# Attention scores from two-part q and k: two heads stacked in the rows of the array, the diagonal mask on TensorE

## Chip, cores and metric

One core of one Trainium2 chip. The metric is the device time of one launch in microseconds (us), median of the runs shown. Engines are named as in the profile: PE (TensorE matmul), PEld (its weight loads), DVE (VectorE), ACT (ScalarE), POOL (GpSimd), SP (the queue that issues the DMAs).

## What is computed

A macaron block on x of shape 8 x 1024 x 256, all float32:

```python
x = x + 0.5 * ffn(layernorm(x))      # fp4-quantised gate, up and down, hidden 704
x = x + attn(layernorm(x))
x = x + 0.5 * ffn(layernorm(x))

def attn(x):                         # 16 heads of 16 columns
    q, k, v = (heads(x @ W.T) for W in (Wq, Wk, Wv))
    logits = einsum('bhqd,bhkd->bhqk', q, k) * 16 ** -0.5
    logits = where(causal, logits, -max)
    return merge(softmax(logits) @ v) @ Wo.T
```

## The kernel before

Stages in order: weights (split into high and low parts), first feed-forward, the q/k/v projection (`project_qkv`, 16 chunks of 512 rows), attention, then output projection and second feed-forward in one pipeline. The change touches the projection's outputs and attention; the feed-forwards are left alone.

**Operands.** q and k are needed at float32 accuracy. The projection writes each as three bf16 parts (`qkv_parts`: ACT rounds the high part, DVE subtracts into `rest`, ACT rounds the middle part, POOL subtracts the low one) to DRAM. For attention `fill` loads a group of 4 heads of one sequence into a `q_stack` and a `k_stack` with 12 DMAs: 6 pairs of parts x 16 = 96 rows, so that one bf16 matmul with 96 contraction rows gives a head's q.k. Rows 96 and 97 hold minus one in `k_stack` and the row maximum in two bf16 parts in `q_stack`, so the 98-row matmul gives q.k minus the maximum. There is a ring of 4 groups' buffers.

**Order.** 8 sequences x 4 groups = 32 groups, run one after the other by `group(b, g, last)`; sequences 1 to 6 are a hardware loop. Each engine has its own instruction stream and waits on counters (`once`, `wait_ge`); PE executes its stream in order. A group has 12 steps (`STEPS`). Step i takes one 128-row tile of keys against up to 512 queries, in widths 512, 384, 256, 128, then 512, 512, 512, 384, 512, 256, 512, 128 columns. In step i PE does:

- S, the scores of the 4 heads (`score_head`, line 1260): the two heads of pair A into the two banks of `hT_ps`, those of pair B into `av_ps`. Each pair has this one buffer, so the next step's S waits until ACT has taken it;
- V, the values of the step before (`values`, line 1283): 4 heads, float32, `probs` against `v_group`, one head in each 32 columns of the array, into `o_ps` (a bank of `gu_ps`);
- U, units of the row maximum (`max_unit`, line 1243) for the group one or two ahead: q.k again, this time queries on the partitions, into one of three banks (two of `gu_ps`, and `xd_ps`) in strict turn: entry e uses bank e mod 3 and waits (`bank_free`) until entry e - 3 has been consumed. A unit is one matmul of up to 512 columns, or several heads side by side when they are narrow. A group has 39 units; step 0 to 11 carry 5, 3, 2, 1, 4, 5, 4, 3, 5, 2, 4, 1 of them. DVE consumes each unit (`reduce_unit`): a masked maximum (line 1436) for blocks on the diagonal, a plain one (line 1441) elsewhere;
- T, the transposes of finished outputs (`turn_out`, after steps 1 and 5) and one of the maxima (`turn_max`, after V in step 7), which take a bank in the same turn. The outputs are consumed by DVE's `one_over` and `divide` (steps 2 and 6), the maxima by ACT's `m_hi` and DVE's `m_lo` (in step 8, behind the first unit).

ACT makes `probs` from the scores (line 1376, one instruction for both heads of a pair).

**Mask on the diagonal.** In steps 0 to 3 PE adds it: one bf16 matmul of `mask_kq` against an identity for each head (line 1264, 16 in a group). In steps 5, 7, 9 and 11 (`DIAG`) ACT copies the 128-column diagonal block of both heads to `diag_scores` (line 1373), POOL masks it (line 1413), ACT takes the exponential (line 1381), and V waits for that too.

**Before group 0** the maxima of group 0 and part of group 1's are made with nothing else on PE (the loop over `FIRST`).

## Time and profile before

| | us |
|---|---|
| median of 3 runs | 2229.68 (2229.11 to 2231.6) |
| the profiled execution | 2228.96 |
| its span, first to last instruction | 2227.2 |
| first feed-forward and weights | to about 560 |
| q/k/v projection | to about 688 |
| attention | to about 1685 |

Busy shares over the span: PE 94%, DVE 86%, PEld 62%, ACT 59%, POOL 45%. The table of 40 slices shows PE in its top tenths almost throughout, a granted clock of 9 tenths or more save in the first slices and in the one at 668 to 724 us (6 tenths), and POOL near idle in attention.

In the rows, "x4" is a number of instructions merged into one row: start, duration, engine, line, operation, tiles, shapes, count. A float32 matmul has two records. Consecutive matmuls overlap in their durations, so what one costs PE in a stream is the distance of its start to the next start.

### The profile page before, as it was taken

Reading aid. Unit: us, or ns where it says so; the run is one execution under the profiler, and the core shown is the slowest. Engines: PE = TensorE matmul, PEld = TensorE weight load, DVE = VectorE, ACT = ScalarE, POOL = GpSimd, SP = SyncE. Lnnn points to the kernel's source line nnn. Section 1 sums busy time; section 2 is a strip of 40 time slices with the busy share of each in tenths; the row PEclk is TensorE's granted clock in tenths of the full one; section 3 lists DMA queues with packets and bytes.
Section 4 is the critical chain, followed back from the end, with each engine's and each line's share of the span. In section 5 each row is a group of like instructions: output and inputs, shape, how many; then the busy total and the mean of one; then the engine's idle time right before and its main releaser. Section 6 shows DMA issues by size and latency. Waiting matters only on the chain. (4 is left out here: it accounts for less than half of the span.)

```text
span 2227.2 us, 50129 instructions
## 1 busy us (share of the span) xinstructions
PE 2087.8 (94%) x13960; PEld 1374.4 (62%) x13960; DVE 1923.9 (86%) x4807; ACT 1313.3 (59%) x2413; POOL 1005.3 (45%) x1671
## 2 busy tenths in 40 slices
PE   4799999997998999999999999999998799999998
PEld 3688888886883333333333333333336788888887
DVE  6799999996987888888888888988863699999996
ACT  3455555543762777777677777777784344555553
POOL 4788888873654011111011111101110288888884
PEclk7899999998996999999999999999998899999998
DMA  6000000002689665545665546665403100000000
GB/s 210 1 1 0 0 0 0 0 1 71 229 234 181 76 78 72 72 65 70 77 78 66 71 63 77 78 78 67 55 12 122 35 16 19 19 19 19 19 19 25
DMA packets 163272, 133.33 MB, mean 60 GB/s; under 512 B 78432, under 2 KB 138208, under 8 KB 163040
## 3 DMA queue, kind: packets, MB, share of 16 engines
q1 hardware_dynamic: 163104, 131.25, 32.8%
q8 instruction: 86, 1.41, 0.3%
q14 instruction: 82, 0.67, 0.1%
HBM read 79.82 MB, written 51.38 MB: 59 GB/s over the span
## 5 line engine op out<-in xcount | busy, mean ns | idle before, releaser
L1413 POOL TENSOR_SCALAR_AFFINE_SELECT diag_scores<-diag_scores 128x256 f32<-128x256 f32 x256 | 104.1, 406 | 876.9 <-ACT diag_scores L1373 870.9
L1436 DVE CUSTOM_DVE_ANT_0 gu_ps<-gu_ps,mask_qk 128x256 f32<-128x256 f32 (+3 forms) x801 | 372.5, 501 | 33.6 <-PE gu_ps L1243 31.6
L1376 ACT ACTIVATE probs<-hT_ps 128x1024 f32<-128x1024 f32 (+3 forms) x352 | 280.4, 796 | 176.4 <-PE hT_ps L1264 112.8
L1243 PE MATMUL gu_ps<-k_stack,q_stack 96*128 96x512 bf16 (+3 forms) x1121 | 327.1, 331 | 9.9 <-DVE part_max L1436 7.4
L1283 PE MATMUL gu_ps<-probs,v_group 128*17 128x512 f32 (+3 forms) x3072 | 323.1, 493 | 0.7 <-ACT probs L1381 0.6
L713 PE MATMUL gu_ps<-wguT_hi,ffn_xT_hi 128*128 128x512 f32 (+1 forms) x768 | 313.1, 408 | 7.2 <-DVE ffn_xT_lo L589 5.1
L1376 ACT ACTIVATE probs<-av_ps 128x1024 f32<-128x1024 f32 (+3 forms) x352 | 282.1, 801 | 22.3 <-PE av_ps L1260 17.6
L713 PE MATMUL gu_ps<-wguT_hi,ffn_xT_lo 128*128 128x512 f32 (+1 forms) x768 | 290.9, 379 | 0.0
L713 PE MATMUL gu_ps<-wguT_lo,ffn_xT_hi 128*128 128x512 f32 (+1 forms) x768 | 290.7, 379 | 0.0
L691 ACT ACTIVATE ffn_z<-xs,ffn_shift,ffn_rstd 128x256 f32 (+1 forms) x128 | 77.1, 602 | 349.8 <-POOL ffn_shift L642 349.8
L1441 DVE TENSOR_REDUCE part_max<-gu_ps 128x1 f32<-128x512 f32 x320 | 208.3, 683 | 62.9 <-PE gu_ps L1243 62.9
L1260 PE MATMUL hT_ps<-q_stack,k_stack 98*128 98x512 bf16 (+3 forms) x768 | 242.3, 331 | 15.9 <-issue 14.1
L1243 PEld LDWEIGHTS gu_ps<-k_stack,q_stack 96*128 96x128 bf16 x1121 | 96.9, 98 | 220.7 <-DVE part_max L1436 149.1
L1260 PE MATMUL av_ps<-q_stack,k_stack 98*128 98x512 bf16 (+3 forms) x768 | 218.0, 329 | 3.1 <-ACT probs L1376 3.1
L744 PE MATMUL xd_ps<-wdT_hi,ffn_hT_hi 128*128 128x256 f32 x640 | 192.9, 301 | 21.7 <-DVE ffn_hT_lo L528 21.7
L612 POOL TENSOR_TENSOR ffn_hq<-ffn_g_h,ffn_nscale 128x704 f32<-128x704 f32 (+1 forms) x256 | 210.4, 843 | 2.8 <-PE hT_ps L755 2.8
L661 POOL TENSOR_TENSOR ffn_v_h<-ffn_h,ffn_rec 128x704 f32<-128x704 f32 x128 | 178.2, 1393 | 16.3 <-DVE ffn_rec L572 6.7
L744 PE MATMUL xd_ps<-wdT_hi,ffn_hT_lo 128*128 128x256 f32 x640 | 182.7, 285 | 0.0
L744 PE MATMUL xd_ps<-wdT_lo,ffn_hT_hi 128*128 128x256 f32 x640 | 182.7, 285 | 0.0
L713 PEld LDWEIGHTS gu_ps<-wguT_hi,ffn_xT_hi 128*128 128x128 f32 x768 | 146.8, 191 | 26.7 <-DVE ffn_xT_lo L589 7.4
L713 PEld LDWEIGHTS gu_ps<-wguT_hi,ffn_xT_lo 128*128 128x128 f32 x768 | 146.1, 190 | 22.6
L713 PEld LDWEIGHTS gu_ps<-wguT_lo,ffn_xT_hi 128*128 128x128 f32 x768 | 147.3, 192 | 17.3
(215 smaller groups left out, 5084.9 us busy)
## 6 DMA issues: line engine op xcount, KB each, us to landing
q_stack<-q_parts SPq DMA_DIRECT2D x192, 128.0 KB, 6.7
k_stack<-k_parts SPq DMA_DIRECT2D x192, 128.0 KB, 7.5
q_parts<-qkv_parts SPq DMA_DIRECT2D x32, 384.0 KB, 2.7
k_parts<-qkv_parts SPq DMA_DIRECT2D x32, 384.0 KB, 2.8
v_ones<-qkv_vst SPq DMA_DIRECT2D x16, 544.0 KB, 3.8
v_group<-v_ones SPq DMA_DIRECT2D x32, 272.0 KB, 10.6
xs<-in_L_attn_x SPq DMA_DIRECT2D x8, 1024.0 KB, 12.0
attn_rows<-ao SPq DMA_DIRECT2D x64, 128.0 KB, 5.4
```

Of the source, the lines that this page charges most:

```text
L612: last = G.tensor_tensor(blocks(hq[:, to:to + n]), blocks(g_h[:, of:of + n]), spread(nscale[:, par, of // BLK:(of + n) // BLK]), ALU.mult)
L661: G.tensor_tensor(blocks(v_h[:, par, :]), blocks(h[:]), spread(rec[:, OF_H]), ALU.mult).then_inc(s["v_h"], 1)
L691: S.activation(z[:, 1 - par, :], x_tile(i + 5), ACT.Identity, bias=shift[:], scale=rstd[:]).then_inc(s["z"], 1)
L713: last = T.matmul(gu_ps[:, n, 0:cols.stop - cols.start], x[:, buf, k * P:(k + 1) * P], w[:, k, cols], start=k == 0 and m == 0, stop=k == K ...
L744: T.matmul(down_ps, x[:, k * P:(k + 1) * P], w[:, k, :], start=k == 0 and n == 0, stop=False)
L1243: mm = T.matmul(out[:, e, :], qs[0:STACK, h0 + e, t * P:(t + 1) * P], ks[0:STACK, h0 + e, c * CHUNK:c * CHUNK + w], start=True, stop=True)
L1260: mm = T.matmul(scores[pair][:, e, 0:widths[i]], ks[0:STACK_MAX, h, t * P:(t + 1) * P], qs[0:STACK_MAX, h, (j + 1) * CHUNK - widths[i]:(j ...
L1283: mm = T.matmul(o_ps[h * VPAD:h * VPAD + VCOLS, CHUNK - w:CHUNK], vs[:, t, h, :], probs[:, h // 2, i % 2, h % 2, 0:w], start=first, stop=last)
L1376: S.activation(probs[:, pair, i % 2, :, first:w], scores[pair][:, :, first:w], ACT.Exp, scale=DH ** -0.5).then_inc(s[pr], 1)
L1413: G.affine_select(out=block_of, in_=block_of, compare_op=ALU.is_ge, fill=MASKED, base=0, pattern=[[0, 2], [1, P]], channel_multiplier=-1). ...
L1436: last = V.tensor_tensor_reduce(out=ps[:, e * w:(e + 1) * w], in0=ps[:, e * w:(e + 1) * w], in1=mask_qk[:, CHUNK - w:CHUNK], scale=1.0, sc ...
L1441: last = V.tensor_reduce(part_max[:, h0:h0 + per, t, c], ps[:, 0:per * w].rearrange("p (h w) -> p h w", h=per), AX.X, ALU.max)
```

## The change

1. q and k are split into two float32r parts (12 and 12 bits) rather than three bf16 ones. A head's stack is 3 pairs of parts x 16 = 48 rows (+2 for the maximum), float32r. ACT rounds the high part and DVE's subtraction writes the low part; the ACT copies of the middle part and POOL's subtractions are gone.
2. Heads 0, 1 of a group lie at partitions 0 to 63 and heads 2, 3 at 64 to 127 (`HALF`). S of a pair and each unit of the maximum are issued as two matmuls that use the upper and the lower 64 rows of the array and write two different banks. `fill` still issues 12 DMAs of 128 KB and one for v, whose DRAM layout now has one run for each partition. The maximum is stored once and loaded with two DMAs.
3. Units come in twos: both entries' banks must be free before the first of the two matmuls. 40 units; steps 0 to 11 carry 2, 2, 1, 0, 3, 2, 2, 2, 2, 1, 2, 1 twos. Their widths, in order, with the number of heads side by side in each unit: step 0: 2 of 128, 512; step 1: 512, 2 of 256; step 2: 512; step 4: 512, 384, 384; step 5: 512, 512; step 6: 512, 512; step 7: 2 of 128, 2 of 256; step 8: 384, 384; step 9: 512; step 10: 512, 512; step 11: 512. The order in a step is S(A), two units, S(B), two units, V, two units, as far as there are any. There are still three banks; two unused entries pad a group to 45.
4. The mask of all eight diagonal steps is added by PE: for each pair four bf16 matmuls (two of 64 and two of 128 columns, each on 64 rows). `diag_scores`, its copies, POOL's masking and the separate exponentials are gone; ACT's one exponential for each pair covers the full width.
5. The minus ones are set on 32 rows of each half by POOL before the stacks are loaded (ring 0 in the weight stage), and SP waits for them before it fills rings 1 to 3.

```diff
-STACK = 6 * DH
+HALF = 64
+STACK = 3 * DH
 STACK_MAX = STACK + 2
...
-                sb(ctx, f"q_stack{r}", [P, GROUP, SEQ], BF16)
+                sb(ctx, f"q_stack{r}", [P, 2, SEQ], F32R)
...
-                    V.tensor_tensor(rest[:, par, j, :], qk_ps[j][:, :], parts[:, par, j, 0, :],
-                                    ALU.subtract).then_inc(s["rest"], 1)
+                    V.tensor_tensor(parts[:, par, j, 1, :], qk_ps[j][:, :], parts[:, par, j, 0, :].bitcast(F32),
+                                    ALU.subtract).then_inc(s["lo"], 1)
...
-                for j in range(4):
-                    qkv_part_done(pool, "mid", c, j, 4)
-                    G.tensor_tensor(parts[:, par, j, 2, :], rest[:, par, j, :], parts[:, par, j, 1, :],
-                                    ALU.subtract).then_inc(s["lo"], 1)
...
-                    per = CHUNK // w if t else 2
-                    UNITS += [(h, per, t, c, w) for h in range(0, GROUP, per)]
+                    per = 2 if 2 * w <= CHUNK else 1
+                    UNITS += [(e, p, per, t, c, w) for p in range(0, 2, per) for e in range(2)]
...
-            SLOTS = {0: (0, 0, 0, 0, 0), 1: (0, 1, 0, 0, 0), 2: (1, 0, 0, 1, 0), 3: (1, 0, 1, 0, 1), 4: (1, 1, 0, 1, 1),
-                     5: (1, 1, 1, 1, 1)}
+            SLOTS = {0: (0, 0, 0), 1: (1, 0, 0), 2: (1, 1, 0), 3: (1, 1, 1)}
...
-                            for e in range(per):
-                                mm = T.matmul(out[:, e, :], qs[0:STACK, h0 + e, t * P:(t + 1) * P],
-                                              ks[0:STACK, h0 + e, c * CHUNK:c * CHUNK + w],
-                                              start=True, stop=True)
-                            mm.then_inc(s["smax"], 1)
+                            for n in range(per):
+                                for e in range(2):
+                                    rows = slice(e * HALF, e * HALF + STACK)
+                                    mm = T.matmul(ps[e][:, n * w:(n + 1) * w], qs[rows, p0 + n, t * P:(t + 1) * P],
+                                                  ks[rows, p0 + n, c * CHUNK:c * CHUNK + w], start=True, stop=True)
+                                    if n == per - 1:
+                                        mm.then_inc(s["smax"], 1)
...
+                            if i in DIAG:
+                                for low, of in ((1, slice(HALF, 2 * HALF)), (0, slice(0, 2 * HALF))):
+                                    for e in range(2):
+                                        rows = slice(e * HALF, (e + 1) * HALF)
+                                        mm = T.matmul(scores[pair][:, e, 0:of.stop - of.start],
+                                                      pick[rows, low * HALF:low * HALF + P], mask_kq[rows, of],
+                                                      start=False, stop=True, skip_group_check=True)
...
                                             bank_free(b, g, at)
-                                            max_unit(*later(b, g, which[0], last), which[1], ps)
+                                            if which[1] % 2:
+                                                max_unit(*later(b, g, which[0], last), which[1],
+                                                         (turn_ps[(at - 1) % BANKS], ps))
...
-                                    if diag is not None:
-                                        first = P
-                                        S.copy(diag_scores[:, pair, diag % 2, :, :], scores[pair][:, :, 0:P]
-                                               ).then_inc(s["taken" if w > P else pr], 1)
...
+                                    S.activation(probs[:, pair, i % 2, :, 0:w], scores[pair][:, :, 0:w],
+                                                 ACT.Exp, scale=DH ** -0.5).then_inc(s[pr], 1)
```

## Rows read from the trace of the kernel before

**Rows 1.** The page: busy time, share of the span, instructions.
```profile
PE 2087.8 (94%) x13960; PEld 1374.4 (62%) x13960; DVE 1923.9 (86%) x4807; ACT 1313.3 (59%) x2413; POOL 1005.3 (45%) x1671
```

**Rows 2.** Busy time by window: start:end, length, engines, granted clock, DMA share, GB/s.
```profile
560.00:700.00 140.00, 134.11 (x769) 111.10 (x767) 117.26 (x259) 87.85 (x159) 88.21 (x82) 0.95 0.80 235
705.00:710.00 5.00, 4.77 (x10) 0.94 (x9) 5.00 (x14) 0.00 (x0) 0.00 (x0) 0.50 1.14 144
1042.50:1072.04 29.54, 29.04 (x221) 11.34 (x218) 26.42 (x86) 22.46 (x42) 3.25 (x8) 1.00 0.55 70
1650.00:1680.00 30.00, 26.62 (x205) 8.17 (x205) 2.19 (x8) 27.50 (x55) 4.88 (x12) 1.00 0.04 11
```

**Rows 3.** Instructions of the tile row_max, one for each group.
```profile
L1450 DVE TENSOR_REDUCE row_max<-part_max x32: 219/220/222, 713.5 to 1650.4; 128x32 f32<-128x64 f32 x32
```

**Rows 4.** PE in order of time in attention, from three steps.
```profile
1161.39 1.05 PE L1283 MATMUL gu_ps<-probs,v_group 128*17 128x512 f32 x8
1162.38 0.39 PE L1243 MATMUL xd_ps<-k_stack,q_stack 96*128 96x512 bf16 x1
1162.61 0.60 PE L1291 MATMUL gu_ps<-ident,o_sb 128*128 128x128 f32 x4
1163.05 0.38 PE L1260 MATMUL hT_ps<-q_stack,k_stack 98*128 98x512 bf16 x1
...
1175.43 0.63 PE L1283 MATMUL gu_ps<-probs,v_group 128*17 128x256 f32 x8
1175.99 0.39 PE L1243 MATMUL gu_ps<-k_stack,q_stack 96*128 96x512 bf16 x1
...
1185.80 0.22 PE L1264 MATMUL hT_ps<-mask_kq,ident_bf 128*128 128x128 bf16 x1
1185.86 0.22 PE L1260 MATMUL hT_ps<-q_stack,k_stack 98*128 98x128 bf16 x1
```

**Rows 5.** PE in the first feed-forward: float32r matmuls, exposed and streamed, and six transposes.
```profile
301.21 0.48 PE L713 MATMUL gu_ps<-wguT_hi,ffn_xT_hi 128*128 128x512 f32 x1
301.53 0.40 PE L713 MATMUL gu_ps<-wguT_lo,ffn_xT_hi 128*128 128x512 f32 x1
301.76 0.39 PE L713 MATMUL gu_ps<-wguT_hi,ffn_xT_lo 128*128 128x512 f32 x1
...
305.93 0.82 PE L755 MATMUL hT_ps<-ident,ffn_hq 128*128 128x128 f32 x6
```

**Rows 6.** All engines in order of time: a unit consumed, its bank refilled.
```profile
1160.36 0.60 DVE L1436 CUSTOM_DVE_ANT_0 gu_ps<-gu_ps,mask_qk 128x384 f32<-128x384 f32 x1
...
1160.88 0.14 DVE L1436 DVE_READ_ACCUMULATOR2_ANT part_max<- 128x1 f32 x1
1160.88 0.69 DVE L1441 TENSOR_REDUCE part_max<-xd_ps 128x1 f32<-128x512 f32 x1
...
1161.08 0.39 PE L1243 MATMUL gu_ps<-k_stack,q_stack 96*128 96x512 bf16 x1
```

**Rows 7.** The same before group 0, where PE has nothing but units, and the first exposed float32r matmul at half clock.
```profile
63.81 0.80 PE L713 MATMUL gu_ps<-wguT_hi,ffn_xT_hi 128*128 128x512 f32 x1 [2.88 <-DVE ffn_xT_lo L589]
...
711.39 0.73 DVE L1436 CUSTOM_DVE_ANT_0 gu_ps<-gu_ps,mask_qk 128x512 f32<-128x512 f32 x1
711.59 0.61 PE L1243 MATMUL xd_ps<-k_stack,q_stack 96*128 96x512 bf16 x1
712.04 0.14 DVE L1436 DVE_READ_ACCUMULATOR2_ANT part_max<- 128x1 f32 x1
```

**Rows 8.** ACT by form, 1650 to 1686 us: count, busy, mean ns of one, idle before.
```profile
L1381 ACT ACTIVATE probs<-diag_scores 128x256 f32<-128x256 f32 x14 | 5.6, 435 | 0.5
```

**Rows 9.** POOL: its memsets of k_stack, and its idle time ahead of the first feed-forward.
```profile
L1399 POOL MEMSET k_stack<- x4: 3506/3506/3507, 688.6 to 699.0; 2x4096 bf16 x4
...
52.27 0.19 POOL L624 TENSOR_TENSOR ffn_eps_var<-ffn_aggr,eps_tile 128x1 f32<-128x1 f32 x1 [8.33 <-DVE ffn_aggr L592]
```

More of the change, by code:

```diff
@@ L280, in _ @@
                     fp4(2)
+                    dve.wait_ge(consts, 8)
+                    V.memset(pick[:, 0:HALF], 0.0)
+                    V.memset(pick[:, 2 * HALF:3 * HALF], 0.0)
+                    V.tensor_tensor(pick[:, HALF:2 * HALF], ident[:, 0:HALF], ident[:, HALF:P], ALU.add)
+                    V.memset(mask_kq[:, 0:HALF], MASKED)
+                    for half in range(2):
+                        rows = slice(half * HALF, (half + 1) * HALF)
+                        V.tensor_copy(mask_kq[rows, HALF:2 * HALF], full_mask[rows, rows])
                 @block.tensor
                 def _(pe):
[L284 removed]
+                    pe.wait_ge(consts, 8)
                     def transposes(q):
@@ L1394, in _ @@
                     def _(pool):
[L1396 removed]
+                        for r in range(1, RING):
                             if r == 2:
                                 qkv_stored(pool)
[L1399 to L1417 removed]
+                            minus_ones(pool, ring[r], s["filled"], 2 * r - 2)
                     @block.vector
```

204 lines of the change are left out of this document (87 added, 117 removed).

## Prediction, made before the changed kernel was run

> **What bounds the kernel now.** I read the busy shares first [rows 1]: PE 94%, DVE 86%. An average over stages says little, so I went on to windows [rows 2]. The feed-forwards are left as they are. The projection has PE busy 134.1 of 140 us, and its PE work stays. What is left is attention, where `row_max` marks each group once: 936.9 us for 31 groups [rows 3], 30.2 us each. An undisturbed group takes 29.54 us (31 x 29.54 = 915.7, so 21 us lie at the hardware loop's ends). In it PE is busy 29.04 us, DVE 26.42, ACT 22.46, POOL 3.25, at the full clock of 2.4 GHz [rows 2]. So PE sets the pace and DVE is 3.1 us behind it. A change that takes work from PE can win at most those 3.1 us, and only if DVE is then always fed. That "if" is the question here.
>
> **How DVE is fed.** DVE's reads of the maximum (U) come out of three banks in turn. Today PE may fill a bank as soon as the unit three before is consumed, so DVE has up to two units in hand while PE does something else. The longest such thing is V: 1161.39 to 1162.38, 0.99 us for 512 columns, and 0.56 for 256 [rows 4]; with a gap of 0.08 ahead of it I take 1.07, 0.86, 0.64, 0.43 for 512, 384, 256, 128. After the change a two takes two banks and needs both free. With three banks that means: the next two may start when the first unit of the last two is consumed, and at that moment DVE has only one unit, about 0.65 us, in hand. Refilling costs: 0.14 us to read the accumulator, 0.06 until PE starts (1161.02 to 1161.08), and the matmul's length [rows 6], for an exposed float32r matmul 0.48 [rows 5]. DVE's masked reads start 0.65 apart for 512 columns [rows 7] and 0.52 for 384 (1160.36 to 1160.88) [rows 6]; on that line 256 take 0.39 and 128 take 0.26, estimates. For 512 columns that is 0.65 + 0.20 + 0.48 = 1.33 us from first unit to first unit, against 1.30 that DVE needs for two units. So there is no slack: every moment that PE is late, DVE stands still, and it can't catch up, as the next two waits for DVE again.
>
> The Trainium skill (TensorEngine Tiling (Array Packing), Restrictions and Gotchas) warns of this side of row tiling: different row tiles must write different PSUM banks, so the pressure on PSUM rises. The trace of before has no row tiles and can't show it. The same page gives 2x as the ceiling of two row tiles; by it alone the score matmuls would halve and attention would end on DVE, which is the second rival below.
>
> **The cost of the new PE work.** S or U of two heads, 512 columns: not in the trace. Float32r matmuls stream at 0.23 us [rows 5], bf16 ones at 0.22 (0.31 from 1161.08 to V at 1161.39, with the gap) [rows 4, 6]. If the two row tiles run side by side the pair costs 0.23; if not, 0.46. The nearest row is V, where four heads on four column tiles take 0.99 us together for eight records of 512 columns, which is side by side [rows 4]; I take 0.24. For narrower ones the two float32 weight loads bind: six transposes with such loads come 0.11 apart ((0.82 - 0.28)/5) [rows 5], so 0.22, or 0.44 for 2 heads side by side. A wait ahead exposes a load: 0.31 rather than 0.23 [rows 5], so +0.06 to 0.1. Masks: 16 matmuls of 0.06 before [rows 4]; after, four bf16 matmuls for each pair in 8 steps, 64 in all. Side by side in twos 0.12 for a pair's four, one after the other 0.24; I take 0.16. T as now: 1162.61 to 1163.05, 0.44 [rows 4].
>
> PE's sum for a group: S 12 x 0.24 + 12 x 0.22 = 5.5, U the same, masks 16 x 0.16 = 2.6, V 6 x 1.07 + 2 x (0.86 + 0.64 + 0.43) = 10.3, T 1.0: 24.9 us, 4.1 below now. But the sum isn't the time.
>
> **The group, two by two.** From one two to the next the time is the larger of PE's work between them (P) and DVE's turn-around (D). D is 1.28 for plain 512, 1.34 for masked 512, 1.20 for 384 (0.52 + 0.20 + 0.48), 1.15 for 2 of 128 (0.52 + 0.20 + 0.43). U is 0.30 after a wait, and 0.20 more with 2 heads side by side; S is 0.40 or 0.38 with its mask. In order:
> - step 0, first to second two: D 1.15; to step 1: D 1.28; within step 1: D 1.28.
> - step 1 to 2: U 0.50 + V 1.07 + T 0.44 + S 0.38 = 2.39.
> - step 2 to 4 (step 3 has no units): U 0.24, S 0.38, V 0.86, S 0.38, S 0.38, V 0.64, S 0.24 = 3.12. DVE has 1.4 us of work there.
> - steps 4 and 5: D 1.28, 1.20, 1.20, 1.28.
> - step 5 to 6: 0.30 + 1.07 + 0.44 + 0.24 = 2.05; within 6: D 1.34.
> - step 6 to 7: 0.30 + 1.07 + 0.38 = 1.75; within 7: D 1.15.
> - step 7 to 8: the maxima's transpose takes a bank, so both units (2 x 0.78) must be consumed: 0.48 + 1.56 + 0.20 = 2.24; within 8, with `m_lo`: 1.30.
> - step 8 to 9: 0.30 + 0.86 + 0.38 = 1.54; 9 to 10: 0.38 + 1.07 + 0.24 + 0.24 = 1.93; within 10: D 1.34; 10 to 11: D 1.34.
> - step 11 to the next group: 0.24 + 0.38 + 1.07 + 0.40 = 2.09.
>
> The 12 entries set by DVE sum to 15.1 (1.30 within step 8 among them), step 7 to 8 is 2.2, the seven others, set by PE, 14.9: 32.2 us, against 29.54 now: +2.6 us. The halved matmuls are spent on waiting: 7 us of each group PE waits for a bank, 6 us DVE waits for PE. Bounds: masks at 0.10 or 0.24 in the ten places where PE's side counts give -0.6 or +0.8; U without the exposed load -0.4; first S after V exposed +0.8. So 31.1 to 33.8 us.
>
> **The sum over the kernel.** 30 groups carry a full set of units: 30 x 2.6 = +79 (bounds +47 and +127). Loop ends stay.
> - Before group 0, DVE never waits now (5.00 of 5.00 us) although the clock is at its half, 1.2 GHz [rows 2]: units come 0.65 apart, PE starts 0.06 after the accumulator is read [rows 7]. After, the exposed matmul is 0.80 at that clock [rows 7]: 0.65 + 0.20 + 0.80 = 1.65 for a two against 1.30, for 20 twos and a few of group 1: +8 (0 if the clock is full there).
> - The last group is ACT's: busy 27.5 of 30 us [rows 2]. Eight separate exponentials of 0.44 [rows 8] and eight copies of about 0.39 go; the wider exponentials give back some 2 us: -4.
> - The projection: ACT, DVE and POOL shed work that PE hides; of 5.9 us without PE some go: -2 (0 to -5). Its stores grow from 6 to 8 bytes for each element while the DMA engines are 80% busy [rows 2], with half as many packets for each byte; if that cover fails, a few us come back.
> - POOL's memsets: 3.5 us for 4096 columns [rows 9], so about 2 for 2048 float32. Two in the weight stage lie in 8.33 us of POOL idle [rows 9]. Two ahead of the fill of ring 1 and four ahead of ring 2's delay loads that are needed 20 us later: 0. The second DMA of the maxima: 0, as scores need it some 10 us later.
>
> +79 + 8 - 4 - 2 = +81 on 2229.0, the profiled execution, which is 0.7 below the median: 2310.
>
> **The rivals.**
> - Coupling is milder than I think and DVE becomes the pace: a group takes DVE's 26.4 and about 1 us of unavoidable gaps, 27.4: -2.1 x 30 = -64, last group and projection -6: 2160. For it: PE's sum of 24.9. Against: the rule of two banks out of three, which is in the code; V alone, 1.07 us, is longer than the 0.65 that DVE has in hand. Halfway cases end between 2160 and 2225. 0.22.
> - The row tiles don't run side by side (the change doesn't do what it says): a pair costs 0.46. It adds some 2.6 in the entries set by PE (twelve matmul pairs of 512 or 384 columns), and masks one after the other 0.8: 35.6 a group, +6.1 x 30 = +183, with the terms above 2415. For it: no row tile in the trace. Against: V's column tiles. 0.10.
> - A fallen clock inside a group would be an addition to the forecast: steps 4 and 5 have PE at work about half the time, and before group 0, with PE streaming about a third of the time, the rows show 1.2 GHz. Doubling one P entry of each group costs 1 to 2 us, 30 to 60 us in all; it is why the range goes up to 2380.
> - Coupling as forecast: 0.63. All of it cancels by chance: 0.05.
>
> **How the numbers follow.** Forecast 2310; its own range 2270 to 2360. Faster by over 0.2% (about what a measurement of this kernel can tell from no change): 0.22; within: 0.05; slower: 0.63 + 0.10 = 0.73. The 8-in-10 range leaves out half of each outer rival: 2180 to 2380.
>
> **What would show it.** `row_max` 32.2 us apart (27.4 in the first rival, 35.6 in the second). PE busy near 25 of 32 us by streams, DVE still 26.4 busy and idle near 6, its idle time ended by PE's units at the head of steps 2, 4, 6, 9 and 0. PE idle ahead of units, released by DVE's maxima. Two matmuls of a pair starting within 0.1 us of one another if row tiles overlap. ACT near 18 us a group, POOL none. I am wrong if DVE idles under 3 us a group.

## The result, and the profile after

| | before | after |
|---|---|---|
| median, us | 2230.32 (2229.11 to 2231.6, 4 runs) | 2526.84 (2504.24 to 2548.18, 4 runs) |
| ratio to before | 1 | 1.128 (95% 1.119 to 1.138) |
| profiled execution, its span | 2228.96, 2227.2 | 2541.1, 2539.3 |
| mean granted clock over the span | 0.963 | 0.855 |

The changed kernel is 12.8% slower. The direction and the smaller of two causes were forecast (2310 us, by a wait for two banks); the size was not, and 2526.84 lies outside the range of 2180 to 2380. Most of what is missing is TensorE's clock. A kernel's executions fall into a faster and a slower state, and the ratio is taken from the faster ones alone: after, from 2541.10, 2512.58, 2504.24 and 2507.33 us (the last isn't in the median).

The page of after: busy time and share of the span (PE, PEld, DVE, ACT, POOL), then two lines of the table of 40 slices. The first line answers to [rows 1].

```profile
PE 2229.0 (88%) x15496; PEld 1473.6 (58%) x15496; DVE 1941.5 (76%) x4813; ACT 1200.5 (47%) x1933; POOL 829.3 (33%) x1354
...
PE   3999999989868888888887898888988789999998
...
PEclk6999999999958776796688857967688999999999
```

PE's busy time has grown by 141 us, though its streams were to shrink by 4 us in each group: it runs at half speed for much of attention. That is the long stretch in the middle where the granted clock has 5 to 9 tenths; before it had 9 in every slice of attention but the first (6) and the last (8).

The instructions of `row_max`, one for each group, answer to [rows 3]:

```profile
L1435 DVE TENSOR_REDUCE row_max<-part_max x32: 219/220/222, 717.2 to 1966.1; 128x32 f32<-128x64 f32 x32
```

31 intervals take 1248.9 us now and took 936.9: +312.0. All the rest nets to nothing: the first `row_max` comes 3.7 us later, and what follows the last takes 3.6 us less (573.2 against 576.8). The sum is the 312.1 by which the spans differ. A group takes 40.29 us on the mean, 10.07 more.

Windows of after (start:end, length, PE, PEld, DVE, ACT, POOL busy, granted clock, DMA share, GB/s): the one group of 31 that has the full clock, one of the longest, the stretch ahead of group 0, and all of attention. They answer to [rows 2].

```profile
1289.49:1322.22 32.73, 26.70 (x269) 11.83 (x267) 27.44 (x86) 19.73 (x28) 0.00 (x0) 1.00 0.46 68
1480.24:1529.01 48.77, 45.14 (x281) 18.86 (x277) 27.84 (x86) 20.55 (x28) 0.00 (x0) 0.53 0.31 46
690.00:725.00 35.00, 15.57 (x51) 7.21 (x49) 26.27 (x84) 1.54 (x2) 4.22 (x3) 0.50 0.75 99
690.00:1980.00 1290.00, 1082.42 (x8284) 459.67 (x8282) 877.95 (x2724) 622.81 (x843) 4.22 (x3) 0.75 0.36 53
```

So the 10.07 us of a group are two things. At the full clock a group takes 32.73 us rather than 29.54: +3.2, 99 us in 31 groups. The other 6.9 us, 213 in all, come with the clock: its mean over attention is 0.75, so half of the time it was at 1.2 GHz. One full-clock group is little to go by, but the three groups at 0.95 (34.2 to 35.0 us) bear it out: a tenth of their time at half speed is worth 1.7 us by my estimate, and without it they take 32.5 to 33.3. At full clock neither PE (26.70) nor DVE (27.44) fills the 32.73 us, as forecast: each waits for the other.

PE and DVE inside that group, PE's rows first:

```profile
1296.51 1.05 PE L1295 MATMUL gu_ps<-probs,v_group 128*17 128x512 f32 x8
1297.49 0.50 PE L1271 MATMUL hT_ps<-q_stack,k_stack 50*128 50x512 f32 x2
1297.83 0.39 PE L1254 MATMUL gu_ps<-k_stack,q_stack 48*128 48x512 f32 x1
1297.83 0.39 PE L1254 MATMUL xd_ps<-k_stack,q_stack 48*128 48x512 f32 x1
1298.06 0.39 PE L1271 MATMUL av_ps<-q_stack,k_stack 50*128 50x512 f32 x2
1299.18 0.49 PE L1254 MATMUL gu_ps<-k_stack,q_stack 48*128 48x512 f32 x2 [0.73 <-DVE part_max L1421]
1299.60 0.63 PE L1295 MATMUL gu_ps<-probs,v_group 128*17 128x256 f32 x8
```

```profile
1298.36 0.70 DVE L1421 CUSTOM_DVE_ANT_0 gu_ps<-gu_ps,mask_qk 128x512 f32<-128x512 f32 x1 [0.47 <-PE xd_ps L1254]
1298.98 0.14 DVE L1421 DVE_READ_ACCUMULATOR2_ANT part_max<- 128x1 f32 x1
...
1299.70 1.29 DVE L1426 TENSOR_REDUCE part_max<-gu_ps 128x1 f32<-128x512 f32 x2
```

The two matmuls of a unit pair start together (1297.83) and the next pair follows 0.23 us later: row tiles run side by side. DVE stands still for 0.47 us until they are done; then PE stands still for 0.73 us until the first of the two is consumed. From DVE's first read of one two (1298.36) to that of the next (1299.70) are 1.34 us, the forecast's D for masked 512. PE starts 0.06 us after the accumulator is read (1298.98 + 0.14 to 1299.18), as in [rows 6]. What is new is the S after V: 0.34 us to the next start (1297.49 to 1297.83), where a pair elsewhere takes 0.23.

### The profile page after: what moved, and what is told of

Read it like the earlier page. It is cut to its first block and busy times, and to the rows that moved or that the text cites. A ratio compares the mean times of both kernels' runs of the same rounds, so it can differ in the third digit from the quotient of the medians.

```text
span 2539.3 us, 51665 instructions
## 1 busy us (share of the span) xinstructions
PE 2229.0 (88%) x15496; PEld 1473.6 (58%) x15496; DVE 1941.5 (76%) x4813; ACT 1200.5 (47%) x1933; POOL 829.3 (33%) x1354
## 5 line engine op out<-in xcount | busy, mean ns | idle before, releaser
L1383 ACT ACTIVATE probs<-hT_ps 128x1024 f32<-128x1024 f32 (+3 forms) x384 | 311.8, 812 | 527.2 <-PE hT_ps L1278 354.5
L1254 PE MATMUL gu_ps<-k_stack,q_stack 48*128 48x512 f32 (+3 forms) x1055 | 360.8, 488 | 163.8 <-DVE part_max L1421 84.6
L1421 DVE CUSTOM_DVE_ANT_0 gu_ps<-gu_ps,mask_qk 128x384 f32<-128x384 f32 (+3 forms) x735 | 345.8, 509 | 171.7 <-PE xd_ps L1254 85.1
L1295 PE MATMUL gu_ps<-probs,v_group 128*17 128x512 f32 (+3 forms) x3072 | 418.8, 624 | 0.0
L1383 ACT ACTIVATE probs<-av_ps 128x1024 f32<-128x1024 f32 (+3 forms) x384 | 310.3, 808 | 51.5 <-PE av_ps L1278 48.8
L1254 PEld LDWEIGHTS gu_ps<-k_stack,q_stack 48*128 48x128 f32 x1055 | 169.6, 229 | 268.0 <-DVE part_max L1421 162.6
L1254 PE MATMUL xd_ps<-k_stack,q_stack 48*128 48x512 f32 (+3 forms) x481 | 235.0, 513 | 34.5 <-DVE part_max L1421 31.8
L1271 PEld LDWEIGHTS hT_ps<-q_stack,k_stack 50*128 50x128 f32 x768 | 85.2, 218 | 238.9 <-issue 184.2
L1271 PE MATMUL hT_ps<-q_stack,k_stack 50*128 50x512 f32 (+3 forms) x768 | 198.3, 512 | 14.4 <-issue 12.6
L1421 DVE CUSTOM_DVE_ANT_0 xd_ps<-xd_ps,mask_qk 128x512 f32<-128x512 f32 (+3 forms) x289 | 150.8, 540 | 52.9 <-PE xd_ps L1254 28.2
L1426 DVE TENSOR_REDUCE part_max<-xd_ps 128x1 f32<-128x512 f32 x192 | 132.1, 688 | 76.6 <-PE gu_ps L1254 67.8
```

The source lines that it names most:

```text
L1254: mm = T.matmul(ps[e][:, n * w:(n + 1) * w], qs[rows, p0 + n, t * P:(t + 1) * P], ks[rows, p0 + n, c * CHUNK:c * CHUNK + w], start=True, s ...
L1271: mm = T.matmul(scores[pair][:, e, 0:widths[i]], ks[rows, pair, t * P:(t + 1) * P], qs[rows, pair, (j + 1) * CHUNK - widths[i]:(j + 1) * C ...
L1295: mm = T.matmul(o_ps[h * VPAD:h * VPAD + VCOLS, CHUNK - w:CHUNK], vs[:, t, h, :], probs[:, h // 2, i % 2, h % 2, 0:w], start=first, stop=last)
L1383: S.activation(probs[:, pair, i % 2, :, 0:w], scores[pair][:, :, 0:w], ACT.Exp, scale=DH ** -0.5).then_inc(s[pr], 1)
L1421: last = V.tensor_tensor_reduce(out=ps[:, e * w:(e + 1) * w], in0=ps[:, e * w:(e + 1) * w], in1=mask_qk[:, CHUNK - w:CHUNK], scale=1.0, sc ...
L1426: last = V.tensor_reduce(part_max[:, half, p0:p0 + per, t, c], ps[:, 0:per * w].rearrange("p (h w) -> p h w", h=per), AX.X, ALU.max)
```

## Experiments

The question after the comparison: what takes the 3.2 us, and why does the clock fall? A first theory, gaps: PE waits for banks, and these gaps bring the clock down. Its rival, work in the array: matmuls on half of the rows bring it down even where PE is always busy. In the texts on record the first is theory 1, the rival is theory 3, and theory 2 is that the waits cost the time by themselves. "Full-clock group" below is the time between two `row_max` in a window whose granted clock is 1.00.

### Pairs or singles (`single`, `single_spread`)

```diff
-                                            if which[1] % 2:
-                                                max_unit(*later(b, g, which[0], last), which[1],
-                                                         (turn_ps[(at - 1) % BANKS], ps))
+                                            max_unit(*later(b, g, which[0], last), which[1], ps)
```

`single` issues each unit as one matmul, which waits for its own bank alone. `single_spread` in addition deals the 40 singles evenly over the steps:

```diff
-            SLOTS = {0: (0, 0, 0), 1: (1, 0, 0), 2: (1, 1, 0), 3: (1, 1, 1)}
+            SLOTS = {1: (0, 1, 0), 2: (0, 1, 1), 3: (1, 1, 1), 4: (1, 2, 1), 5: (2, 2, 1), 6: (2, 2, 2)}
```

> The changed kernel with each unit of the maximum issued by itself, as soon as its own bank is free, rather than in twos; order and all else kept. It takes away the rule that two of three banks must be free. Theory 1: DVE is fed earlier, groups at the full clock 29 to 31 us apart, but PE's streaming stays near 25 us of them, so the clock may still fall in places: kernel 2250 to 2450. If the rule of two banks were not what makes DVE wait (a rival: PE's order is), groups at full clock stay at 32.7 and the kernel within 1% of the changed one.

> The changed kernel with units issued singly, and spread as evenly as in the kernel before: two ahead of V, one behind it, in a step of four. Against the run called single (31.2 us a group at the full clock, 35.4 in the mean): DVE has a unit in hand across V, so 30 to 30.8 at the full clock. If the clock follows the amount of array at work, it falls as in single or more, since units that aren't issued side by side occupy half the array: mean group 33 to 37 us, kernel 2310 to 2430.

Measured: `single` 2379.57 us (ratio to before 1.066, 1.063 to 1.068), `single_spread` 2318.84 (1.042, 1.038 to 1.048). Windows of a full-clock group of `single` and of one of those at a low clock:

```profile
1350.97:1382.15 31.18, 28.84 (x271) 13.46 (x269) 26.62 (x87) 19.65 (x27) 0.00 (x0) 1.00 0.48 71
1417.18:1461.33 44.15, 40.42 (x269) 18.38 (x265) 26.92 (x87) 20.21 (x27) 0.00 (x0) 0.65 0.34 51
```

and 30 us of `single_spread`:

```profile
1440.00:1470.00 30.00, 28.62 (x270) 14.36 (x273) 26.59 (x88) 19.44 (x28) 0.00 (x0) 1.00 0.49 74
```

PE works 2 us more without the side-by-side units (28.84 against 26.70), and the group is 1.55 us shorter. Spread evenly it is 30.1 us (the median of 20 such groups), 0.6 above before. So of the 3.2 us at full clock the wait for two banks of three is 1.55, net of the overlap that singles give up, and the uneven dealing in twos 1.1; what the halved matmuls save doesn't show in the group, even with most waits gone. And with fewer waits the clock's share sinks too, from 7.6 us a group to 4.3 and 2.9. Both kernels came out as expected, `single` 0.2 us above its range for the group.

### One unit less in hand, in the kernel before (`less_ahead`, `none_ahead`)

Before a unit starts, the unit two entries back (`less_ahead`), or the one just before it (`none_ahead`), must be consumed, rather than the one three back. Nothing else of the kernel before is changed.

```diff
                                             bank_free(b, g, at)
+                                            if ENTRIES[at - 2][0] == "unit" and later(b, g, ENTRIES[at - 2][1], last):
+                                                of = b * GROUPS + g - (1 if at < 2 else 0) + ENTRIES[at - 2][1]
+                                                once(pe, "reduced", of * NU, ENTRIES[at - 2][2] + 1)
                                             max_unit(*later(b, g, which[0], last), which[1], ps)
```

> The kernel before with one wait added: a unit may start only when the unit two before is consumed (rather than three), so that DVE has one unit less in hand, as with twos. bf16, 96 rows, no row tiles. It measures the coupling by itself. Theory 2: groups from 29.54 to 31 to 33 us, kernel 2275 to 2340, clock still over 0.93 as PE's matmuls are the full ones. If the clock falls with these gaps alone (theory 1), kernel over 2400 with clock under 0.9. If DVE's stock of units doesn't matter: 2229.

> The kernel before, in which a unit starts only when the unit right before it has been consumed, so that DVE has nothing in hand. At 2.4 GHz: 39 turn-arounds of 0.20 us and a matmul of 0.2 to 0.45 us each are exposed, 16 to 25 us on top of DVE's 26.4, less where PE has its own work to do meanwhile: a group takes 40 to 50 us, and PE is idle for 10 to 20 us of it, more than in any group of the changed kernel. If gaps bring the clock down, the granted clock of such groups is below 0.9, the groups take 50 to 75 us and the kernel over 2850 us. If full-height matmuls keep it up in spite of gaps, the groups between loop ends show 1.00 as the 34.0 us ones did, and the kernel takes 2550 to 2800 us.

Measured: `less_ahead` 2378.19 us (1.067, 1.065 to 1.069), `none_ahead` 3162.91 (1.418, 1.415 to 1.420). The first costs more than the 31 to 33 us and 2275 to 2340 us that I gave it. A group of `less_ahead`, then a stretch of `none_ahead`:

```profile
1208.00:1242.01 34.01, 30.82 (x217) 10.92 (x217) 27.38 (x88) 23.03 (x43) 3.21 (x8) 1.00 0.48 64
```

```profile
1200.00:1260.00 60.00, 46.71 (x211) 12.75 (x211) 28.01 (x84) 23.19 (x40) 3.25 (x8) 0.64 0.29 37
```

One unit less in hand costs 4.5 us a group with the same streams: the wait is a sufficient cause for what the changed kernel loses at full clock. The clock mostly bears gaps of 3.2 us in 34 when the matmuls have 96 and more rows: it is full in 19 of 31 groups (27 before), 0.91 or 0.95 in 11 and 0.72 in the first. With nothing in hand PE is idle 13.3 of 60 us and the clock is 0.64 (0.59 to 0.84 in all 31 groups), though no matmul of q.k is on half of the rows: large gaps alone do bring the clock down, as the first theory expected.

### Useless work in the gaps (`fill`, `fill_48`)

In 11 places of a group PE does two matmuls of 512 columns ahead of the wait, whose result is overwritten; with 128 rows in `fill`, with 48 in `fill_48`.

```diff
+                                            if which[1] % 2 and (i, (which[1] - units_of[i][0][1]) // 2) in FILLED:
+                                                for _ in range(2):
+                                                    T.matmul(turn_ps[(at - 1) % BANKS], neg_ident[:, :],
+                                                             wguT[0][:, 0, 0:CHUNK], start=True, stop=True)
                                             bank_free(b, g, at)
```

> The changed kernel with useless work added: in eleven places of each group (ahead of the wait for the second bank of a two, where the two before was issued with little PE work between) PE runs two extra 512-column float32r matmuls on all 128 rows, into the bank that is free and is overwritten next. 22 x 0.23 = 5 us of extra PE streaming for a group. Theory 1 (PE's gaps let the granted clock fall, and the clock is most of the loss): clock of attention back near 1.0, groups 33 to 35 us apart rather than 40.3, the kernel at 2300 to 2370, faster than the changed kernel although it does more. Theory 2 (the waiting for banks alone costs it): groups no shorter, 40 to 43 us, kernel 2530 to 2620. Theory 3 (row-tiled float32r matmuls lower the clock whatever the gaps): clock stays near 0.75 and the time is 2550 or more.

> The same 22 useless matmuls for a group as in the run called fill, of the same 512 columns and in the same places, but on 48 of the 128 rows instead of all. PE streams exactly as long as in fill, where the clock came back to 0.96 and the kernel to 1.088 of the one before. Theory 1 (the clock follows PE's gaps): the same as fill, 2420 us, clock 0.96. Theory 3 (the clock follows how much of the array works, as the run called same_half suggests, where PE streamed without gaps on 48 and 50 rows and the clock stayed at 1.2 GHz): clock near 0.75, kernel 2600 to 2900, as the fillers then only cost.

Measured: `fill` 2423.47 us (1.088, 1.086 to 1.091), `fill_48` 2394.94 (1.076, 1.072 to 1.079). A group of `fill`:

```profile
1376.16:1410.87 34.71, 33.70 (x291) 15.11 (x289) 27.46 (x87) 19.82 (x28) 0.00 (x0) 1.00 0.42 64
```

Work that serves nothing makes the changed kernel 103 and 132 us faster. The full-clock group grows (34.7 and 33.5 against 32.73), but 20 and 17 of 31 groups have the full clock, where one had it. The difference between the mean and the full-clock group falls from 7.6 to 1.7 and 1.9 us: the clock is what the changed kernel lost most by, and it can be had back. `fill` is dearer than I expected (2300 to 2370 us). Between the two, `fill_48` speaks for the first theory: fillers on 48 rows bring the clock back as well as full ones (2394.94 us, where the rival gave 2600 to 2900). But the fillers close gaps and add work to the array alike, so this doesn't rule out that the height matters too.

### Half of the rows without gaps (`same_half`, `same_half_fill`)

Both matmuls of each pair read rows 0 to 63, so nothing runs side by side; heads 2 and 3 get wrong scores. `same_half_fill` has the fillers of `fill` too.

```diff
-                                    rows = slice(e * HALF, e * HALF + STACK)
+                                    rows = slice(0, STACK)
```

> The changed kernel with the second matmul of every pair (scores, units, masks) read from the same partitions 0 to 63 as the first, so that two heads of four get the other heads' scores (that part of the result is left out); the two can no longer run side by side in the array. Everything else, the twos of banks too, stays. Theory 1 (gaps let the clock fall): PE streams some 11 us more for a group, so clock higher than 0.75, and by my own sum of the second rival 35.6 us for a group at the full clock: the kernel at 2400 to 2450, faster than the changed one though its matmuls don't overlap. Theory 2 (waiting alone) or theory 3 (the form of the matmul): 43 us or more for a group, kernel 2600 or more.

> The changed kernel with both matmuls of each pair reading rows 0 to 63 (so the right scores of heads 2 and 3 are left out), as in the run in which PE was busy 57.56 of 57.95 us of a group at 1.2 GHz, and in addition the 22 useless 512-column matmuls of 128 rows in each group. If the clock falls because of PE's gaps, the fillers close none here, since there are none: they only add 22 x 0.45 us = 10 us to each group at 1.2 GHz, and the kernel takes about 3102.8 + 30 x 10 = 3400 us. If the clock stays low because matmuls on half of the rows leave too much of the array idle, the fillers bring the full clock back: a group that took 57.9 us at 1.2 GHz takes about 58/2 + 22 x 0.23 + 22 x 0.20 for switches of row mode, 36 to 42 us, and the kernel is faster than without them although it does more: 2450 to 2650 us.

Measured: `same_half` 3102.82 us (1.394, 1.390 to 1.398), `same_half_fill` 3162.78 (3086.52 to 3171.04, so whether the fillers made it slower on the whole is unclear). A group of `same_half`, and two stretches of about a group of `same_half_fill`:

```profile
1295.12:1353.07 57.95, 57.56 (x269) 30.82 (x265) 27.72 (x87) 20.80 (x27) 0.00 (x0) 0.56 0.26 39
```

```profile
1376.00:1420.00 44.00, 43.69 (x297) 23.34 (x294) 28.30 (x89) 20.52 (x27) 0.00 (x0) 1.00 0.35 50
2271.00:2346.00 75.00, 75.00 (x295) 38.33 (x292) 27.81 (x88) 20.79 (x27) 0.00 (x0) 0.53 0.20 30
```

PE is busy for 57.56 of 57.95 us and the clock is 0.56 (0.50 to 0.62 in all 31 groups): gaps are not needed for a low clock. This is the rival's outcome; the first theory gave 2400 to 2450 us. The Trainium skill (TensorE: Matmul & The Clock Gate, What's actually happening) says that the clock is set by how busy PE has been recently. By the busy time that the profile shows, this group should have had the full clock; the measurement decides, and PE's busy share is no guide to the clock here.

Both expectations for `same_half_fill` missed. Seven of its 31 groups have the full clock and take 43.5 us, near the 36 to 42 that I gave for it; the others keep a low one and take up to 75 us. The fillers can bring the clock back but don't do it reliably, and where they don't they cost double.

### How many rows, and changes between row counts (`u48`, `u66`)

In the kernel before, the units contract 48, or 66, of the 96 rows (some of the six products are left out of the maximum); waits and columns are the same.

```diff
-                                mm = T.matmul(out[:, e, :], qs[0:STACK, h0 + e, t * P:(t + 1) * P],
-                                              ks[0:STACK, h0 + e, c * CHUNK:c * CHUNK + w],
+                                mm = T.matmul(out[:, e, :], qs[0:48, h0 + e, t * P:(t + 1) * P],
+                                              ks[0:48, h0 + e, c * CHUNK:c * CHUNK + w],
```

> The kernel before with one edit: the units of the row maximum contract over 48 of the 96 rows (three of the six products are left out there, so the maximum is that of slightly coarser scores), everything else as before; each matmul streams the same columns in the same time. Theory 1 (gaps): no change, 2229 us, clock 0.96. Theory 3 (amount of array at work): the clock of attention falls below 0.9 and the kernel goes over 2300, with no wait and no instruction changed.

> The kernel before, its units of the maximum contracting 66 of the 96 rows (the maximum leaves out two of the six products and part of a third or so; streams, waits and shapes of outputs are the same, and 66 rows need the whole array as 96 do). If the 18% that 48 rows cost at full clock was the switch between matmuls on half of the rows and on all of them, an undisturbed group is 29.5 us again, within 0.2. If it was the number of rows itself, it is between 29.5 and 35.0, about 32. For the clock: if fewer rows at work slow its return after a loop's end, the groups there are longer than the 32 to 36 us of the kernel before, and the median is 2240 to 2300; if rows don't matter within the whole array, the median is 2229, within 0.2%.

Measured: `u48` 2479.17 us (1.107, 1.100 to 1.113), `u66` 2243.59 (1.0061, 1.0044 to 1.0078). PE at full clock, S and U of 512 columns in turn: first before, with 98 and 96 rows, then `u48`, with 98 and 48:

```profile
1160.17 0.38 PE L1243 MATMUL xd_ps<-k_stack,q_stack 96*128 96x512 bf16 x1
1160.39 0.39 PE L1260 MATMUL av_ps<-q_stack,k_stack 98*128 98x512 bf16 x1
1160.61 0.38 PE L1243 MATMUL gu_ps<-k_stack,q_stack 96*128 96x512 bf16 x1
```

```profile
1309.36 0.39 PE L1260 MATMUL hT_ps<-q_stack,k_stack 98*128 98x512 bf16 x1
1309.69 0.39 PE L1243 MATMUL gu_ps<-k_stack,q_stack 48*128 48x512 bf16 x1
1310.01 0.39 PE L1260 MATMUL hT_ps<-q_stack,k_stack 98*128 98x512 bf16 x1
1310.33 0.39 PE L1243 MATMUL xd_ps<-k_stack,q_stack 48*128 48x512 bf16 x1
```

Three windows of `u48`, and an undisturbed group of `u66`:

```profile
763.00:821.00 58.00, 58.00 (x228) 13.57 (x228) 30.01 (x90) 24.23 (x43) 3.25 (x9) 0.54 0.27 38
1820.00:1850.00 30.00, 29.76 (x190) 9.48 (x189) 24.03 (x76) 19.87 (x34) 2.44 (x6) 1.00 0.04 10
1851.00:1902.00 51.00, 51.00 (x192) 11.78 (x185) 24.38 (x63) 19.38 (x33) 2.44 (x6) 0.50 0.02 6
```

```profile
1366.00:1395.55 29.55, 29.05 (x225) 11.31 (x217) 26.45 (x86) 22.45 (x43) 3.24 (x9) 1.00 0.57 73
```

A matmul follows another of a different height after 0.32 us, rather than 0.22: a change between half of the rows and all of them costs 0.10 us. In `u48` this makes the group 34.97 us; with 66 rows, which need the whole array as 96 do, it is 29.55 again, so it is the change and not the number of rows. The Trainium skill (TensorEngine Tiling (Array Packing), Key Properties) has this as "Mode switching requires drain", without a price; the trace agrees, and the price is 0.10. PE's busy time doesn't show it: 58.00 of 58.00 us are busy in the window at clock 0.54.

The rival's forecast of over 2300 us came true, but mostly by a price that neither theory has. Of the 250 us by which the 31 intervals of `u48` are longer, 168 are the changes at full clock (5.4 us a group); the clock has the rest, 2.6 us a group. And its last two windows show the clock going down without a gap: from 1820 to 1850 us it is full and PE is idle 0.24 us, from 1851 to 1902 it is 1.2 GHz and PE is never idle. Stalls are not what takes the full clock away there. Whether it is the height of the units or the changes around them, the run doesn't say.

`u66` is 0.6% slower. Its 31 intervals are 15.8 us longer: 13.6 in the five groups behind the ends of the hardware loop (35.3 to 37.1 us, where before has 32.2 to 35.8), the rest in the first one. So a little of the clock's return seems to hang on the height of the matmuls even inside the whole array.

### The masks (`pe_masks`)

The kernel before with `DIAG = []`: all masks on PE (128-row matmuls), no copies to `diag_scores`.

```diff
-            DIAG = [i for i, (j, t) in enumerate(STEPS) if j and t >= 4 * j]
+            DIAG = []
```

> The kernel before with one part of the change alone: the masks of all eight diagonal steps on PE as one bf16 matmul for each head (16 more for a group), no copies, no POOL masking, no separate exponentials; three bf16 parts and 96 rows as before. My sum: +16 x 0.06 = 1.0 us of PE for a group, less what ACT's shorter chain gives back: groups 29.6 to 30.6 us, kernel 2230 to 2262, clock unchanged near 0.96. If ACT's detour over POOL had held PE up, groups under 29.5 and the kernel under 2225.

Measured: 2251.78 us (1.0106, 1.0089 to 1.0123), 30.27 us for each full-clock group against 29.54. Where PE sets the pace, 16 more mask matmuls cost 0.73 us, 0.05 each. The clock stays (0.965). So the masks on PE don't break the clock by themselves; these have 128 rows, and the changed kernel's 64-row ones stand in no run alone.

### Which useless matmuls bring the clock back (`spread_boost`, `boost_48`, `before_boost`, `before_boost_48`)

One useless matmul of 512 columns ahead of each of the 24 units in steps 0 to 6, in the first group of each sequence alone. The first two stand on `single_spread`, the others on the kernel before; `spread_boost` and `before_boost` have 128 rows, `boost_48` the 48 rows of the unit's own half, `before_boost_48` rows 0 to 47.

```diff
                                             bank_free(b, g, at)
+                                            if g == 0 and i < 7:
+                                                T.matmul(ps, neg_ident[:, :], wguT[0][:, 0, 0:CHUNK],
+                                                         start=True, stop=True)
```

> The changed kernel with its units issued singly and spread evenly over the steps (2318.8 us), with one useless 512-column matmul of 128 rows ahead of each unit in steps 0 to 6 of each sequence's first group alone. An undisturbed group stays at 30.0 us. If a fallen clock comes back only when more of the array is at work, the groups behind the loop's end, 39 to 45 us now, shorten to 34 to 38 and the median to 2270 to 2295. If the fillers merely take PE's time, each of eight sequences grows by about 20 x 0.25 us = 5 us and the median is 2350 to 2360.

> Units issued singly and spread evenly (2318.8 us), with one useless 512-column matmul ahead of each unit in steps 0 to 6 of each sequence's first group, as in the run of 2560.5 us, where those groups took 66 to 69 us at a clock of 0.6, but here the useless matmul reads 48 rows of the unit's own half, so that it adds no change of row mode. If changes of mode hold the clock down, these groups are much shorter, 38 to 46 us, and the median 2300 to 2370. If matmuls on half of the rows hold it down by themselves, the clock stays low for all of the group: at 1.2 GHz the fillers cost 24 x 0.43 us = 10 us on top of 44, the group takes 52 to 58 us, and the median is 2430 to 2480.

> The kernel before, with one useless 512-column matmul of 128 rows ahead of each unit in steps 0 to 6 of each sequence's first group: no changes of row mode, PE wholly busy. Both theories expect a full clock within these groups soon after the loop's end: about 25 fillers x 0.23 us = 5.7 us on top of 32 to 36, so 37 to 42 us for each such group, and 2229 + 8 x 5.7 = 2275 us, 2260 to 2300.

> The kernel before, with one useless 512-column matmul of 48 rows ahead of each unit in steps 0 to 6 of each sequence's first group, between matmuls of 96 and 98 rows. Each adds two changes of row mode, 0.2 us at full clock and 0.3 to 0.6 at half. If changes of mode hold the clock down, these groups stay at 1.2 GHz: 29.5 x 2 + 25 x (0.43 + 0.5) = 75 us or so each, at least 60, and the median is 2480 to 2580. If only the share of half-height matmuls matters (about a quarter of PE's time here), the clock returns nearly as in the kernel with 128-row fillers: 42 to 50 us for such a group, and the median 2300 to 2360.

| on | filler | median, us | groups behind a loop end, us | their clock |
|---|---|---|---|---|
| `single_spread` | none | 2318.84 | 39.0 to 44.7 | 0.62 to 0.78 |
| `single_spread` | 48 rows, same half | 2410.18 | 49.5 to 51.7 | 0.64 to 0.66 |
| `single_spread` | 128 rows | 2560.53 | 67.2 to 69.2 | 0.59 to 0.61 |
| before | none | 2230.08 | 32.2 to 35.8 | 0.90 to 1.00 |
| before | 128 rows | 2284.96 | 40.5 to 40.8 | 0.96 |
| before | 48 rows | 2434.37 | 50.1 to 63.4 | 0.65 to 0.86 |

The profile of `boost_48` (second line) is of the longest of its four executions, 2444.8 us; that of `before_boost_48` (last line) is of the shortest of its five, 2384.3 us, so its groups are shorter here than in the median.

PE of `spread_boost` in such a group, and windows of the same place in `spread_boost` and `before_boost`:

```profile
1064.83 0.80 PE L1338 MATMUL gu_ps<-wguT_hi,neg_ident 128*128 128x512 f32 x1
1065.56 0.79 PE L1253 MATMUL gu_ps<-k_stack,q_stack 48*128 48x512 f32 x1
...
1066.78 0.80 PE L1338 MATMUL xd_ps<-wguT_hi,neg_ident 128*128 128x512 f32 x1
1067.51 0.79 PE L1253 MATMUL xd_ps<-k_stack,q_stack 48*128 48x512 f32 x1
```

```profile
1042.00:1111.00 69.00, 64.83 (x293) 28.98 (x289) 28.78 (x86) 20.26 (x28) 0.00 (x0) 0.60 0.21 33
```

```profile
1222.00:1263.00 41.00, 37.66 (x245) 15.74 (x241) 28.04 (x87) 23.21 (x42) 3.44 (x9) 0.96 0.45 59
```

`spread_boost` missed both of its expectations, 2270 to 2295 and 2350 to 2360 us: the filler was to bring the clock back or to cost its own time, and the clock stayed down for almost the whole group. A filler of 128 rows among units of 48 adds two changes of height, and at 1.2 GHz a change costs more: 0.73 us from filler to unit, of which 0.43 are 512 columns. Without the changes (`boost_48`) the groups are some 18 us shorter, yet their clock is low all the same, and the 9 us left of what the filler adds are about 24 x 0.43, its own columns at 1.2 GHz: matmuls of half the height don't bring the clock back either. `boost_48` ended between its two expectations, nearer to the one that blames the half height. In the kernel before, the same filler with 128 rows came out as expected: it has the clock at 0.96 and costs 0.28 us each (36.4 against 29.7 us in the first group with fillers that has the full clock throughout); with 48 rows it costs 0.50 each (41.75), which is two changes more, and behind the loop's ends the clock comes back later in all five groups, in one only at 0.65 on the mean. There the expectation that blames changes was right in direction only: it had at least 60 us for each such group and a median of 2480 to 2580, and four take 50 to 51.5, with a median of 2434.37; the other expectation, 2300 to 2360, missed too.

## Why the prediction was right and wrong

What a group costs beyond its full-clock time says where the clock's share sits:

| kernel | mean group, us | full-clock group, us | difference | PE idle in the latter, us |
|---|---|---|---|---|
| before | 30.22 | 29.54 | 0.7 | 0.5 |
| `u66` | 30.73 | 29.55 | 1.2 | 0.5 |
| `less_ahead` | 35.30 | 34.01 | 1.3 | 3.2 |
| `pe_masks` | 30.99 | 30.27 | 0.7 | 0.65 |
| `fill` | 36.38 | 34.71 | 1.7 | 1.0 |
| `fill_48` | 35.49 | 33.6 | 1.9 | 1.5 |
| `single_spread` | 32.98 | 30.1 | 2.9 | 1.4 |
| `u48` | 38.28 | 34.97 | 3.3 | 0.25 |
| `single` | 35.43 | 31.18 | 4.3 | 2.3 |
| after | 40.29 | 32.73 | 7.6 | 6.0 |

- **The coupling of DVE and PE by two banks of three**: right, in kind and size. Forecast 32.2 us a group, measured 32.73; forecast 7 us of PE idle and 6 of DVE, measured 6.0 and 5.3. `single` and `less_ahead` show it from either side. The warning of the Trainium skill (TensorEngine Tiling (Array Packing), Restrictions and Gotchas), that row tiles raise the pressure on PSUM, is what happened; the ceiling of 2x that the same page gives (Theoretical Speedup) was reached by the pair (0.23 us for two matmuls) and not by the kernel.
- **Pairs side by side at 0.24**: right, 0.23. The rival of row tiles that don't overlap is refuted by the starts, and `same_half` shows what that would have been: 3103 us, at a clock that the rival's own figure, 2415, left out.
- **DVE sets the pace**: refuted; DVE is idle 5.3 us. `single_spread` is as near as it came, 30.1 us a group with DVE busy 26.6 of 30.0.
- **The missing 0.5 us at full clock**: the first S after V takes 0.34, not 0.24, and U before V 0.42, not 0.38 (0.30 and the gap of 0.08). I had put +0.8 for that S into the bounds as an exposed load. It equals the 0.10 of a change of height that `u48` shows; V uses all the rows, S and U half. That V's neighbours pay the same price is read from the equal size, not tested by itself.
- **Masks**: forecast 0.16 for a pair's four. They took 0.07 to the next unit (1295.80 to 1295.87) and 0.19 to the next V (1300.86 to 1301.05), with V's gap in it. Right on the mean.
- **Ahead of group 0**: forecast +8, measured +9 (DVE's first instruction of attention is 5.4 us earlier, 683.34 against 688.72, the first `row_max` 3.7 later), at 1.2 GHz, as in [rows 2, 7].
- **Projection -2**: -5.4, a little beyond its bound of -5. **Last group -4**: what follows the last `row_max` is 3.6 shorter.
- **The clock**: the step that failed. The sum of 2310 put it at nothing, and none of the chances was set aside for it; it stood in the text as a possible addition of 30 to 60 us, one P entry doubled in each group, and only there. It was 213 us. Two things were wrong. First, I looked for it only where PE stands still (steps 4, 5 and ahead of group 0). The row that I had [rows 2] spoke against that: from 705 to 710 us PE is busy for 4.77 of 5.00 us at a clock of 0.50. I read it as PE streaming a third of the time (0.22 of 0.65 us), which holds for matmuls at the full clock alone. The runs show two ways to 1.2 GHz: large gaps with full-height matmuls (`none_ahead`, 0.64), and half-height matmuls with almost no gaps (`same_half`, 0.56; `u48` from 1851 us on, 0.50). A third, changes of height, is likely and not shown by itself: in `spread_boost` fillers of full height, each with two changes, left the clock low for longer than no fillers did, but among units of half height. The changed kernel has all of these. Second, I doubled one entry. When the clock falls, all of PE's work doubles: in the 48.77 us group PE is busy for 45.14 us, no longer behind DVE but the bound, for the whole group. A price for a fallen clock has to be a whole group at half speed times the number of groups, not one step.

What stays open: how the 213 us divide between gaps, half height and changes. The full-clock group of after is one of 31, so neither its gaps nor its half-height matmuls can be taken away alone without changing the other. `less_ahead`, idle 3.2 us a group with full-height matmuls, has the full clock in 19 of 31 groups, and `single`, idle 2.3 us with half-height ones, in 8: there the height, or the changes around V that come with it, made the difference. For the 6.0 us of idle time in the changed kernel there is no run with full height whose gaps are spread as there. The nearest are two groups of `less_ahead` (37.04 and 37.09 us) with PE idle for 6.2 us at a clock of 1.00 throughout, and the group behind each is at 0.95; but 3.0 of the 6.2 us are a single gap at the loop's end.

No version here beats the kernel before. The nearest with two-part q and k is `single_spread`, 4.2% behind; its full-clock group is 0.6 us longer than before's, the rest is the clock (2.9 us a group, against 0.7).

## What to carry over

Before sharing banks, count what the consumer has in hand while the producer does its longest other thing; if a pair of units must wait for two of three banks, the saved matmul time comes back as waiting. Treat the granted clock as something a change can break: PE's busy share doesn't say whether it will hold, and halving the rows that matmuls use or adding gaps put it at risk, and mixing heights costs time for each change, whatever the clock. When a clock may fall, price it as all of the stage's TensorE work at half speed.

## What the runs showed of the hardware that I had not expected

- A change between matmuls on half of the rows and on more costs 0.10 us at 2.4 GHz (0.32 between starts, not 0.22). At 1.2 GHz it is 0.11 to 0.14 for bf16 and 0.30 for float32r (0.73 against 0.43), loads included.
- TensorE stays at 1.2 GHz while its busy time is 99 to 100% of a group: 57.56 of 57.95 us in `same_half`, with 48 and 50 rows in all q.k matmuls, and 58.00 of 58.00 in `u48`, with 48 rows in the units alone. In `u48` it even goes down to 1.2 GHz at full busy time, with 0.24 us of idle time in the 30 us before.
- Useless matmuls can make a kernel faster: 22 in each group, 103 us less. The same kind of matmul, dealt singly between others of a different height, made another kernel 242 us slower.
- Contracting 66 rather than 96 rows in the units, with no stream or wait changed, costs 0.6%, all of it where the clock comes back: after a loop's end and in the first group.
